# Four chunks of a graph-network layer's aggregation as two 64-row tiles of TensorE, summed by VectorE

## What is computed

```python
def _cxin_conv(x, a, eps, W, b):
    ax = a @ x
    h = ax + (1.0 + eps[0]) * ax
    for i in range(3):
        h = relu(h @ W[i].T + b[i])
    return h

h = maximum(_layernorm(x), 0.0)
out1 = _cxin_conv(h, adj, eps1, W1, b1)
out2 = _cxin_conv(x2, adj, eps2, W2, b2)
return x + concatenate((out1, out2), axis=1) @ Wm.T + bm
```

## Time and profile before

| | |
|---|---|
| median of 3 runs | 404.85 us (404.8 to 405.64) |
| the profiled execution | 404.87 us |
| its span in the trace | 403.3 us |
| TensorE busy | 399.4 us, 99% of the span |
| DVE busy | 219.6 us, 54% |
| ACT busy | 220.4 us, 55% |
| mean granted TensorE clock | 0.999 of full speed |

### The profile page before, as it was taken

How to read it: one execution, slowest core, us unless ns; L and a number is a source line. 1 busy time by engine, 2 the same in 40 slices (tenths; PEclk the granted TensorE clock), 3 DMA queues, 4 the chain that set the end, 5 groups by cost and what they waited for, 6 DMA issues and landing times.

```text
span 403.3 us, 4833 instructions
## 1 busy us (share of the span) xinstructions
PE 399.4 (99%) x1757; PEld 327.0 (81%) x1757; DVE 219.6 (54%) x267; ACT 220.4 (55%) x258; POOL 8.4 (2%) x19
## 2 busy tenths in 40 slices
PE   8999999999999999999999999999999999999997
PEld 3788888888888888888888888888888888888886
DVE  5898878656464434551645517345373444755223
ACT  6876868557574533555433556334564335766034
POOL 0000000000000000000100001000000000000100
PEclk9999999999999999999999999999999999999999
DMA  8998883744645165334574336653175551740100
GB/s 301 420 403 338 310 327 142 297 154 152 236 154 198 53 244 203 108 119 197 172 296 160 119 137 228 240 207 132 76 260 208 208 193 42 264 179 2 52 0 28
DMA packets 14030, 76.22 MB, mean 189 GB/s; under 512 B 1920, under 2 KB 2176, under 8 KB 6080
## 3 DMA queue, kind: packets, MB, share of 16 engines
q1 hardware_dynamic: 12240, 71.18, 46.9%
q0 software_dynamic: 1200, 3.93, 2.9%
q10 hardware_dynamic: 576, 0.92, 0.7%
HBM read 73.93 MB, written 2.10 MB: 189 GB/s over the span
## 4 chain that ended last, share of the span: by engine, by line
PE 99%; DVE 0%; issue 0%; DVEq 0%
PE acc L590 24%; PE acc L586 24%; PE acc L587 24%; PE second_acc L587 3%; PE second_acc L586 3%; PE second_acc L590 3%; PE hidden L590 3%; PE hidden L586 3%; PE hidden L587 3%; PE second_acc L604 2%; PE acc L604 2%; PE merged L756 1%; PE acc L618 1%; PE merged L590 1%; PE merged L586 1%; PE merged L587 1%
## 5 line engine op out<-in xcount | busy, mean ns | idle before, releaser
L586 PE MATMUL acc<-adj_hi,feat_lo 128*128 128x512 f32 x432 | 168.0, 389 | 0.0
L587 PE MATMUL acc<-adj_hi,feat_hi 128*128 128x512 f32 x432 | 168.0, 389 | 0.0
L590 PE MATMUL acc<-adj_lo,feat_hi 128*128 128x512 f32 x432 | 168.0, 389 | 0.0
L423 DVE TENSOR_TENSOR adj_lo<-adj_raw,adj_hi 128x2048 fp32r<-128x2048 f32 x48 | 108.4, 2289 | 37.5 <-ACT adj_hi L264 36.6
L264 ACT ACTIVATE adj_hi<-adj_raw 128x2048 fp32r<-128x2048 f32 x48 | 90.3, 1924 | 17.3 <-PE acc L590 15.4
L429 DVE TENSOR_TENSOR act_lo<-act_f,act_hi 128x512 fp32r<-128x512 f32 x60 | 41.1, 691 | 104.4 <-ACT act_f L284 104.3
L587 PEld LDWEIGHTS acc<-adj_hi,feat_hi 128*128 128x128 f32 x432 | 81.1, 188 | 16.9
L590 PEld LDWEIGHTS acc<-adj_lo,feat_hi 128*128 128x128 f32 x432 | 81.1, 188 | 16.9
L586 PEld LDWEIGHTS acc<-adj_hi,feat_lo 128*128 128x128 f32 x432 | 81.1, 188 | 16.7
L283 ACT ACTIVATE act_hi<-hidden,bias 128x512 fp32r<-128x512 f32 x45 | 30.9, 688 | 95.5 <-PE hidden L590 95.5
L483 DVE TENSOR_TENSOR adj_lo<-adj_raw,adj_hi 128x2048 fp32r<-128x2048 f32 x14 | 31.7, 2290 | 5.4 <-ACT adj_hi L302 5.4
(11 more groups left out here) (82 smaller groups left out, 224.1 us busy)
## 6 DMA issues: line engine op xcount, KB each, us to landing
adj_raw<-adj_tiles SPq DMA_DIRECT2D x62, 1024.0 KB, 5.3
x_rows<-x_tiles SPq DMA_DIRECT2D x16, 256.0 KB, 7.3
x_res<-x_t POOLq DMA_DIRECT2D x8, 256.0 KB, 6.1
out_t<-y_sb POOLq DMA_DIRECT2D x7, 256.0 KB, 2.3
adj_raw<-adj_second SPq DMA_DIRECT2D x2, 512.0 KB, 6.5
adj_raw<-adj_first ACTq DMA_DIRECT2D x3, 256.0 KB, 4.4
w_raw<-w_t SPq DMA_DIRECT2D x1, 512.0 KB, 5.6
adj_raw<-adj_first SPq DMA_DIRECT2D x1, 256.0 KB, 5.0
```

What stands on the lines that cost most here:

```text
L423: nc.vector.tensor_tensor(adj_lo[:, u % RING, :], adj_raw[:, u % RING, :], f32(adj_hi[:, u % RING, :]), ALU.subtract).then_inc(lo_made, 1)
L586: nc.tensor.matmul(out, lhs_lo, rhs_hi, start=start, stop=False)
L587: nc.tensor.matmul(out, lhs_hi, rhs_hi, start=False, stop=False)
L590: return nc.tensor.matmul(out, lhs_hi, rhs_lo, start=False, stop=stop)
```

## The change

In chunks 3 to 6 (`TILED`) the helper `aggregate` is replaced with `tiled_aggregate`. Each matmul over 128 rows becomes two over 64 rows (`TILE_ROWS`): tile 0 takes partitions 0 to 63 of features and matrix and adds up in `acc[b]`, tile 1 takes partitions 64 to 127 and adds up in `second_acc[b]`. Both still have 512 columns. A full sum is the sum of the two banks. Dense layers and merges stay as they were, over all 128 rows.

ACT no longer reads `acc[b]` for such a chunk. It reads `second_acc[b]`, scaled, into `act_f` (`tiled_operand`), DVE adds the scaled `acc[b]` (`add_tiles`), ACT then signals `act_f_made[b]` and copies `act_f` from SBUF into `act_hi`. Chunk 3's turn is written out ahead of the loop on ACT and DVE, since the chunk before it is not tiled.

```diff
+            def tiled_operand(m, b):
+                src, how = source(m, 0, b)
+                nc.scalar.activation(act_f[:, b, :], tile_acc[1][b][:, :], **how).then_inc(lower_read[b], 1)
+                act.wait_ge(tiles_added[b], m - TURN)
+                act.sem_inc(act_f_made[b], 1)
+                nc.scalar.activation(act_hi[:, b, :], act_f[:, b, :], ACT.Copy).then_inc(act_hi_made[b], 1)
...
+            def add_tiles(m, b):
+                dve.wait_ge(lower_read[b], m - TURN)
+                nc.vector.scalar_tensor_tensor(act_f[:, b, :], tile_acc[0][b][:, :], ax_scale[:, b:b + 1], act_f[:, b, :],
+                                               ALU.mult, ALU.add).then_inc(tiles_added[b], 1)
...
+            def tiled_aggregate(c, u, b):
+                if u == 0:
+                    pe.wait_ge(act_f_made[b], (c - 1) * STEPS + 1)
+                pe.wait_ge(hi_made, c * U + (u + 1))
+                for j in range(JB):
+                    s, cols = columns(u, j)
+                    block = u * JB + j
+                    for k, (feat, adj) in enumerate(((feat_lo, adj_hi), (feat_hi, adj_hi), (feat_hi, adj_lo))):
+                        if j == 0 and adj is adj_lo:
+                            pe.wait_ge(lo_made, c * U + (u + 1))
+                        for t in range(TILES):
+                            rows = slice(t * TILE_ROWS, (t + 1) * TILE_ROWS)
+                            last = nc.tensor.matmul(tile_acc[t][b][:, :], feat[rows, b, block, :], adj[rows, s, cols],
+                                                    start=(u == 0 and j == 0 and k == 0),
+                                                    stop=(u == U - 1 and j == JB - 1 and k == 2))
+                signal(u, b, last)
...
             with pe.Fori(TURN + 1, LAST) as c:
                 for u in range(U):
                     for b in BRANCH_ORDER:
-                        aggregate(c, u, b)
+                        tiled_aggregate(c, u, b)
```

More of the change, by code:

```diff
@@ L58, in gnn_layer_kernel @@
     TURN_OPERAND_AFTER = {3: (0, 2), 4: (0, 3), 5: (1, 0), 6: (1, 1), 7: (1, 2)}
+    TILED = range(TURN + 1, CHUNKS - 1)
+    TILES = 2
+    TILE_ROWS = P // TILES
     LAST = CHUNKS - 1
@@ L127, in gnn_layer_kernel @@
         second_acc = [bank(f"second_acc{b}") for b in range(2)]
+        tile_acc = [acc, second_acc]
         hidden_quarter = [hidden[0], second_acc[0], hidden[1], second_acc[1]]
@@ L166, in gnn_layer_kernel @@
         merged_done = sem("merged_done")
+        lower_read = [sem(f"lower_read{b}") for b in range(2)]
+        tiles_added = [sem(f"tiles_added{b}") for b in range(2)]
         y_made = sem("y_made")
@@ L278, in source @@
                 return (second_acc if isinstance(m, int) and m == 1 else acc)[b], dict(func=ACT.Identity, scale=ax_scale[:, b:b + 1])
+            def tiled_operand(m, b):
[4 more added lines that the diff above has]
+                nc.scalar.activation(act_hi[:, b, :], act_f[:, b, :], ACT.Copy).then_inc(act_hi_made[b], 1)
             def branch_operand(m, k, b):
+                if k == 0 and (not isinstance(m, int) or m in TILED):
+                    tiled_operand(m, b)
+                    return
                 src, how = source(m, k, b)
@@ L383, in _ @@
             operand(1, STEPS - 1)
-            with act.Fori(TURN + 1, LAST) as c:
+            for u in range(U):
+                high_of_unit(TURN + 1, u)
+                if u in OPERAND_AFTER:
+                    operand(TURN, OPERAND_AFTER[u])
+            with act.Fori(TURN + 2, LAST) as c:
                 for u in range(U):
@@ L424, in low_of_unit @@
                                         ALU.subtract).then_inc(lo_made, 1)
+            def add_tiles(m, b):
+                dve.wait_ge(lower_read[b], m - TURN)
+                nc.vector.scalar_tensor_tensor(act_f[:, b, :], tile_acc[0][b][:, :], ax_scale[:, b:b + 1], act_f[:, b, :],
+                                               ALU.mult, ALU.add).then_inc(tiles_added[b], 1)
             def low_of_branch(m, k, b):
+                if k == 0 and (not isinstance(m, int) or m in TILED):
+                    add_tiles(m, b)
                 dve.wait_ge(act_hi_made[b], m * STEPS + (k + 1))
@@ L553, in _ @@
             result(1)
-            with dve.Fori(TURN + 1, LAST) as c:
+            for u in range(U):
+                low_of_unit(TURN + 1, u)
+                if u in OPERAND_AFTER:
+                    low_of_operand(TURN, OPERAND_AFTER[u])
+            result(TURN)
+            with dve.Fori(TURN + 2, LAST) as c:
                 for u in range(U):
```

## The result

The changed kernel takes 415.85 us (median of four runs, 415.39 to 416.47) against 404.94 us (404.8 to 405.64): a ratio of 1.0265, 95% interval 1.0252 to 1.0278. It is 10.9 us slower. The forecast was 410.8 us, slower by 5.9, with a range of 400.0 to 421.5.

The account below looks back on a forecast made before the run. TensorE was taken to bound the kernel: number of matmuls times the 226.6 ns between starts. From 404.87 us, pairs 0, boundaries +4.0 and entries +1.9 gave +5.9, 410.8 us; range 400.0 to 421.5.

Parts of the forecast that it names:

- term 2: Chunk boundaries into chunks 4 to 7: TensorE waits 0.99 us each for DVE's late addition, +4.0 us (3.2 to 4.6).
- term 3: Entering and leaving tiles: one weight load, 0.11 us, lost in each of 17 runs of pairs, +1.9 us.
- Term 1: Aggregation in four chunks: 768 full matmuls become 768 pairs, each costing the same 226.6 ns, so zero change.
- the lower by the loads: Lower bound for pairs: two weight loads 110 ns apart make 220 ns a pair, -5.1 us over 768.
- the upper of 240 ns: Upper bound for overlapping pairs: a load and matmul every 120 ns, 240 ns a pair, +10.3 us.
- the sign that the prediction had set: First matmul after or of a layer: 227 ns from predecessor means no loss, 340 the stagger, 389 or more running out.
- The rival of "running out": Last matmul runs out at each of 34 changes between full array and tiles: forecast plus 5.5 us, 416.3 us; chance 0.13.
- 408 to 416: The forecast case's own range in us, with boundaries at 3.2 to 4.6 us and entries at 0 to 5.5; chance 0.28.
- the covered gap: Second tile covers the 13.3 ns not streaming, pairs about 217 ns: 402.4 us without entry losses; chance 0.24.
- loads that set the pace: Weight loads make each aggregation pair cost 240 ns, +10.3 us, total 421.1 us; chance 0.14.
- tiles that take turns: The two tiles do not overlap in the aggregation: +174 us, near 585 us, or +115 us; chance 0.08.
- The rival on code: Loop body grows from 216 to 408 matmuls; if no longer held, three turns begin with a code load, some us.

Follow-up runs that it names:

- the lone tile: Changed kernel without the second tile's matmuls in the four tiled chunks, rows 64 to 127 left out of these sums: 468.87 us (434.43 to 469.77).
- 409.38: Changed kernel with dense layers and merges inside TensorE's loop also issued as pairs of 64-row matmuls, half of these sums left out: 409.38 us, ratio 1.0104.
- 405.68: Changed kernel with in-loop dense layers and merges as pairs, and DVE's branch 1 addition moved behind unit 0's low part: 405.68 us, ratio 1.001.
- 413.23: Changed kernel with DVE's addition for branch 1 placed behind the low part of unit 0 instead of unit 1: 413.23 us, ratio 1.0194.

## Why the prediction was right, and where it was off

The direction and the range held, and both causes of loss are real; the size of the loss was 5.9 us forecast against 10.9 measured. The measured parts are 0 for the pairs, 2.9 for the boundaries and 8.0 for the changes of shape. That the forecast missed by only 5.0 us is in part luck: term 2 was 1.1 us too large while term 3 was 6.1 too small. Step by step:

- **Term 1, pairs at 226.6 ns: right.** 0.5 us over 864 pairs, with an entry and an exit in it. The reason given, that each tile is a stream of 512-column matmuls with its own load, is what the lone tile shows. Of the bounds, the lower by the loads (two for each pair, 110 ns apart) and the upper of 240 ns rested on loads that queue. They don't: both start within 0.01 us.
- **Term 2, the boundary: right in its cause, 4.0 us forecast and 3.7 measured where it stands alone** (409.38 - 405.68), but 2.6 to 2.9 in the changed kernel (415.85 - 413.23, or 10.9 - 8.0). DVE's way from the result to the operand was 5.07 us at the boundary shown here, as read before, and 5.17 at the next one (246.90 to 252.07). These two rows of the changed kernel are the start and the end of it:

```profile
195.36 0.75 DVE L473 SCALAR_TENSOR_TENSOR y_sb<-merged,bias,x_res 128x512 f32<-128x512 f32 x1 [4.73 <-PE merged L627]
...
200.43 0.74 DVE L453 SCALAR_TENSOR_TENSOR act_f<-acc,ax_scale,act_f 128x512 f32<-128x512 f32 x1
```

What the sum missed is that its terms touch. DVE's 5.07 us run from the merge, and between merge and boundary TensorE now also pays the entry into unit 7, 0.21 us and a few slow matmuls behind it, which is time in which DVE catches up. Two delays on two engines that run side by side from a common point don't add.
- **Term 3, entries and exits: the mis-sized term.** 1.9 us forecast, 8.0 measured. The step that failed is "tile 1's first matmul starts one load after tile 0's, 0.11 us, lost once in each run". There is no such stagger. By the sign that the prediction had set (227 ns no loss, 340 the stagger, 389 the running out) the first distance behind a change, 0.32 us, would have passed for the stagger; only the one after it, 0.34 us, and the starts side by side tell them apart. What is lost is the cover of the weight load, at the way in and at the way out, 34 times 0.2 us and the slow matmuls behind. The count of 17 runs and 34 changes was right. The rival of "running out" named the place; its price was 0.11 + 2 x 0.162 = 0.43 us an excursion, near the 0.47 measured (the four turns of the profiled executions, 203.3 us against 195.8 with the boundaries gone, give 0.44), although its picture (the last matmul's 389 ns run out) is not quite the row's: the load starts 0.32 us after the last matmul's start, inside its record. The prediction's sum also let this term reach only 5.5 us, where its own bound was 1.9 + 5.5 = 7.4; the 8.0 measured lie above both, so its 408 to 416 holds 415.85 only just.

By that rival's price the forecast would have been 416.3 us. It had a chance of 0.13. The Trainium skill, "TensorEngine Tiling (Array Packing)", Tiling Modes, gives the rule that a change of mode drains TensorE and a change of tile does not. The trace agrees in substance: 0.2 us at each change from 128 to 64 rows or back, nothing from tile to tile.

The other rivals: the covered gap (402.4), loads that set the pace (421.1) and tiles that take turns (585) are out by the distances of 0.23 us and the starts side by side. The rival on code is out too. In 200 to 350 us of the changed kernel the only queue with instructions is this one, with two packets where the earlier trace rows has one:

```profile
q14 instruction: 2, 0.02, 0.0%
```

Two small slips of the prediction change nothing: its cases for "slower" leave 0.63 rather than 0.61, and two loads of 0.19 us in full would cost 118 us, not 115.

## What to carry to other kernels

Row tiles with the same number of columns did not beat the full array here: each tile streamed all 512 of them at the same distance of 227 ns, so two tiles of 64 rows are one matmul of 128 for the price of one. They cost at each change of shape, here 0.2 us, because the weight load loses its cover; group tiled work and count the changes before the matmuls. And when a sum needs one more step by an in-order engine, look at what that engine does at that moment: half idle on average, DVE was busy for 5 us at each of the four boundaries, and moving one instruction gave 2.6 to 2.9 us back.

## What the runs showed of the hardware beyond that

- With matmuls over half the rows only, the granted clock fell to the 1.2 GHz level behind two chunk boundaries and stayed there for 24 and 92 us, while TensorE was busy without a pause. The same stream with its second tile kept 2.4 GHz, though its boundaries are as long (distances of 0.75 to 0.95 us). The missing second tile is the only difference between the two programs, so it is what lets the clock fall; what part the pause at the boundary plays was not tried, and neither was why one of the four executions was slowed far less (434.43 us).
- Matmuls of different row tiles don't start in program order. One starts past three waiting matmuls of the other tile. The Trainium skill, "TensorE: Matmul & The Clock Gate", Part 3, says that matmuls start in program order; here the fourth in the program started 0.33 us before the second.
- Weight loads of two row tiles start at the same time to 0.01 us (149.89 and 149.89 in the timeline). So do the matmuls in 719 of the 768 pairs; in one stretch, from 255.6 to 263.8 us, they lie 0.05 us apart. By contrast, two loads into the same rows were 110 ns apart.
